# Graph products between the gate products of an LSTM, and a Householder step without z

## What is computed

```python
x = x + L0(h, adj)   # two linear layers with batch norms over all tokens
# L1: two graph convolutions, then four LSTMs with windows of p = 1, 2, 3, 4 nodes
h = relu(einsum('ts,bsh->bth', adj, x @ Wg0 + bg0))
h = relu(einsum('ts,bsh->bth', adj, h @ Wg1 + bg1))
for p in range(1, 5):
    last = lstm_last(Wih[p-1], Whh[p-1], bih[p-1], bhh[p-1], windows of p nodes of h)
    h = h.at[:, idx, :].set(last)      # the last node of each window
# L2: features through the eigenvectors of the 64 x 64 normalized Laplacian
_, U = eigh(L_norm)
out = U @ (relu((U.T @ features) @ W1 + b1) @ W2 + b2)
# L3: three convolutions with adj * adj
```

## Time and profile before

| | us |
|---|---|
| median of 3 runs (lowest, highest) | 1040.38 (1039.38, 1042.43) |
| the profiled execution | 1039.46 |
| its span, first to last instruction | 1037.7 |
| mean granted clock of TensorE | 0.939 |
| busy: PE / PEld / DVE / ACT / POOL | 862.0 / 573.9 / 585.2 / 528.8 / 333.5 |
| chain that ended last, share of the span | PE 57%, DVE 26%, POOL 7%, ACT 6%, issue 3% |

### The profile page before, as it was taken

One profiled execution on the slowest core, in us unless ns is written; L12 is line 12 of the kernel. 1 busy time (PEld: TensorE's weight loads), 2 busy tenths in 40 slices (PEclk: granted clock), 3 DMA queues, 4 the chain that ended last, 5 costly groups with the idle time before them and its releaser, 6 DMA issues.

```text
span 1037.7 us, 12401 instructions
## 1 busy us (share of the span) xinstructions
PE 862.0 (83%) x3721; PEld 573.9 (55%) x3721; DVE 585.2 (56%) x3105; ACT 528.8 (51%) x962; POOL 333.5 (32%) x404
## 2 busy tenths in 40 slices
PE   2678487498879899798857858896899999999998
PEld 1444233353558546684435723575756857857856
DVE  5899867876865877488997886202503303303101
ACT  1466365375464755657526445455545545545531
POOL 1333101016555266525736316674301201201000
PEclk9999889598899999999978889998899999999999
DMA  7000000000000000000000000000000100100101
GB/s 322 0 2 1 0 0 1 1 1 1 1 1 1 1 0 2 1 1 1 0 0 1 1 1 1 1 0 1 1 1 1 41 1 1 42 0 1 42 1 40
DMA packets 2963, 13.32 MB, mean 13 GB/s; under 512 B 465, under 2 KB 465, under 8 KB 2641
## 3 DMA queue, kind: packets, MB, share of 16 engines
q1 hardware_dynamic: 2896, 12.54, 3.0%
HBM read 8.35 MB, written 4.19 MB: 12 GB/s over the span
## 4 chain that ended last, share of the span: by engine, by line
PE 57%; DVE 26%; POOL 7%; ACT 6%; issue 3%; DMA 0%; SPq 0%; DVEq 0%; ACTq 0%; POOLq 0%
PE PS L401 56%; POOL BIG L881 6%; DVE ST L1530 2%; ACT T L784 2%; DVE stats L1502 1%; ACT BIG L823 1%; DVE Fq L1322 1%; DVE seg L1323 1%; ACT T L773 1%; ACT BIG L815 1%; DVE T L1626 1%; DVE mv L1509 1%; POOL sc L861 1%; DVE sc L1063 1%; DVE vcol L1060 1%
## 5 line engine op out<-in xcount | busy, mean ns | idle before, releaser
L401 PE MATMUL PS<-BIG,wts 128*128 128x512 f32 (+2 forms) x1264 | 443.2, 507 | 41.7 <-POOL BIG L881 21.3
L401 PEld LDWEIGHTS PS<-BIG,wts 128*128 128x128 f32 x1264 | 244.4, 198 | 207.4 <-issue 123.7
L881 POOL TENSOR_TENSOR BIG<-BIG 128x256 f32<-128x256 f32 (+2 forms) x272 | 255.3, 944 | 273.2 <-ACT BIG L815 208.0
L815 ACT ACTIVATE BIG<-PS,lbias 128x256 f32<-128x256 f32 (+2 forms) x312 | 166.1, 559 | 125.7 <-PE PS L401 124.6
L1641 DVE TENSOR_TENSOR X<-X,PS 128x512 f32<-128x512 f32 x64 | 43.5, 683 | 148.7 <-PE PS L401 87.1
L722 ACT ACTIVATE BIG<-PS 128x1024 f32<-128x1024 f32 x64 | 65.5, 1024 | 88.5 <-PE PS L401 88.5
L722 ACT ACTIVATE T<-PS 128x512 f32<-128x512 f32 x96 | 55.3, 593 | 100.5 <-PE PS L401 100.3
L730 ACT ACTIVATE T<-X,shift,rstd 128x128 f32<-128x128 f32 x192 | 78.3, 481 | 43.7 <-DVE shift L1518 43.7
L401 PE MATMUL PS<-T,wts 128*128 128x512 f32 x192 | 97.3, 637 | 0.7 <-ACT T L722 0.4
L1663 DVE TENSOR_TENSOR T<-PS,wts 128x512 f32<-128x512 f32 x16 | 11.1, 692 | 150.6 <-PE PS L401 150.6
L869 POOL TENSOR_SCALAR rstd<-mv 128x4 f32<-128x4 f32 x48 | 10.9, 228 | 225.3 <-DVE mv L1509 225.3
(11 more groups left out here) (303 smaller groups left out, 1154.3 us busy)
## 6 DMA issues: line engine op xcount, KB each, us to landing
X<-x_in SPq DMA_DIRECT2D x1, 4096.0 KB, 12.6
...
```

The lines of the kernel that those rows point to most:

```text
L401: return nc.tensor.matmul(o, l, r, start=start, stop=stop)
L815: nc.scalar.activation(LB[:, q, {"i": I_, "g": G_, "f": F_, "o": O_}[g], 0:n], PS[:, 3 * q + rank[q] % 3, 0:n], ACT.Tanh if g == "g" else ...
L881: nc.gpsimd.tensor_tensor(out, a, b, op).then_inc(pool_set[q], 1)
```

## The change

1. In L1 there is no graph stage behind the first one any more. The products of iteration i+1, and the turns of h of iteration i-1, are single tasks between the gate products of iteration i, at places given by the table TASKS (round, set, half): after the second gate, or behind the last. All tasks use one PSUM bank, `task_bank`, and each waits until the one before has been emptied. h has a second tile for odd iterations (H1).
2. bn and norm are cut into pairs of chunks, at rounds 0 and 4 (SCALED, NORMED), ahead of the tanh of the cell. In the last iteration the norm of L2's first chunks stands there (LAST_NORMED), with its statistics and roots.
3. The first LayerNorm of L1 takes its roots on GpSimd, chunk by chunk, and VectorE does it ahead of its first reflection of this part. The last turn of h is done behind the first products of L2, into the odd banks.
4. A reflection forms neither z nor the row sum with the finished v: the row sum is formed with the unfinished v beside the inverse root (ax) and corrected by beta; the factors for the next row and for S come from scalars.
5. The planner's paces are PACE_AV 7.2 (8.0), PACE_GRID 50, 38 (40, 32), PACE_TWIST 32 (27), PACE_SCAN 15 (13). SHORT_ROUND is gone.

The tables:

```diff
+TASKS = {
+    (0, 1, 1): ("turn", 0), (1, 0, 0): ("turn", 1), (1, 0, 1): ("turn", 2), (1, 1, 0): ("turn", 3),
+    (2, 0, 1): ("turn_h", 0), (2, 1, 1): ("turn_h", 1), (3, 0, 0): ("turn_h", 2), (3, 0, 1): ("turn_h", 3),
+    (4, 1, 1): ("agg", 0), (5, 0, 0): ("agg", 1), (5, 0, 1): ("agg", 2), (5, 1, 0): ("agg", 3),
+    (5, 1, 1): ("g0", 0), (6, 0, 0): ("g0", 1), (6, 0, 1): ("g0", 2), (6, 1, 0): ("g0", 3),
+    (6, 1, 1): ("agg2", 0), (7, 0, 1): ("agg2", 1), (7, 1, 1): ("agg2", 2), (8, 0, 0): ("agg2", 3),
+    (8, 0, 1): ("g1", 0), (8, 1, 1): ("g1", 1), (9, 0, 1): ("g1", 2), (9, 1, 1): ("g1", 3),
+}
+NORMED = {(4, 0): (0, 1), (4, 1): (2, 3)}
+SCALED = {(0, 0): (0, 1), (0, 1): (2, 3)}
+LAST_NORMED = {(9, 1): (0, 1), (10, 0): (2, 3)}
+LAST_ROOTS = 7
+DONE_BY = {"turn": "add", "turn_h": "add_h", "agg": "aggT", "g0": "bias0", "agg2": "aggT2", "g1": "bias1"}
...
-PACE_AV = 8.0
-PACE_GRID = [40.0, 32.0]
-PACE_TWIST = 27.0
-PACE_SCAN = 13.0
+PACE_AV = 7.2
+PACE_GRID = [50.0, 38.0]
+PACE_TWIST = 32.0
+PACE_SCAN = 15.0
```

TensorE:

```diff
+            def task(j, name, k):
+                if held[0]:
+                    before, what, c = held[0]
+                    if what in ("agg", "agg2"):
+                        pe.wait_ge(act_done[c], C_ACT.at(before, DONE_BY[what]))
+                    else:
+                        pe.wait_ge(dve_done[c], C_DVE.at(before, DONE_BY[what]))
+                product(j, name, k, task_bank)
+                held[0] = (j, name, k)
...
-                        for g in gates(s):
+                        for at, g in enumerate(gates(s)):
...
                                 pe.wait_ge(act_set[q], R_ACT.at(i, rank[q][m - 3]))
+                            elif i:
+                                pe.wait_ge(act_set[q], R_ACT.at(i - 1, LAST_GATES[m]))
...
                             spend(n * 4 * (2 if s else 1.25) / 2400)
-                        if s == 0 and p > 2:
-                            spend(SHORT_ROUND)
-                        if r and turned < NK and i + 1 < ITER:
-                            turn(i + 1, turned)
-                            turned += 1
-            for k in range(NK):
-                turn(0, k)
-            spend(8.0)
+                            if at == 1 and 0 in todo:
+                                task(*todo[0])
+                        if 1 in todo:
+                            task(*todo[1])
...
+            for name in ["turn"] + GRAPH:
+                for k in range(NK):
+                    if name == "agg":
+                        pe.wait_ge(dve_done[k], C_DVE.at(0, "add"))
+                    product(0, name, k, l1_bank(k))
+                spend(STARTED if name == "turn" else GAP)
...
                 lstm(i)
-                spend(GAP)
-                for k in range(NK):
-                    pe.wait_ge(pool_set[k // 2], R_POOL.start(i + 1))
-                    for t in range(TPC):
-                        j = nc.tensor.transpose(l1_bank(k)[:, t * P:(t + 1) * P],
-                                                by_tile_of_set(k)[:, t, :], ident)
-                    j.then_inc(pe_done[k], 1)
-                    spend(0.5, i, k, "turn_h")
...
                     else:
-                        for c in range(NK):
-                            pe.wait_ge(dve_done[c], C_DVE.end)
+                        for q in range(2):
+                            pe.wait_ge(act_set[q], R_ACT.start(ITER))
                     tiles(bank(k), k, T0[:, k, :], BDU[:, :])
+                if i == 0:
+                    pe.wait_ge(dve_done[NK - 1], C_DVE.end)
+                    for k in range(NK):
+                        product(ITER - 1, "turn_h", k, odd_bank(k))
```

ScalarE:

```diff
                             rank[q] += 1
+                            if at == 0:
+                                for j, name, k in late:
+                                    after(j, name, k, task_bank)
+                                late = []
+                            for half, j, name, k in tasks(i, r, q):
+                                if name in ("agg", "agg2") and at == (2 if half == 0 else len(gates(s)) - 1):
+                                    after(j, name, k, task_bank)
+                        late = [(j, name, k) for _, j, name, k in tasks(i, r, q) if name in ("g0", "g1")]
+                        if i + 1 < ITER:
+                            for k in SCALED.get((r, q), ()):
+                                bn(i + 1, k)
+                            for k in NORMED.get((r, q), ()):
+                                norm(i + 1, k)
+                        else:
+                            for k in LAST_NORMED.get((r, q), ()):
+                                norm_tiles(0, k, "norm", D_DVE.at(0, "shift"), C_PE.at(ITER - 1, "agg2"))
                         act.wait_ge(pool_set[q], R_POOL.at(i, f"c{r}" if s else f"ig{r}"))
                         nc.scalar.activation(LB[:, q, I_, 0:n], LB[:, q, CELL, 0:n], ACT.Tanh).then_inc(act_set[q], 1)
+                assert not late
...
-            for k in range(NK):
-                norm_tiles(0, k, "norm", D_DVE.at(0, "shift"), C_PE.end)
```

The reflection on VectorE:

```diff
-                z = eb(1)[:, 0:NODES - 1 - k]
-                first = op(v.scalar_tensor_tensor(trail, z, vn, trail, ALU.mult, ALU.add))
-                yield
+                first = op(v.scalar_tensor_tensor(trail, eb(2)[:, 0:NODES - 1 - k], vn, trail, ALU.mult, ALU.add))
+                yield first
                 dve.wait_ge(hh_ops, first)
-                op(v.scalar_tensor_tensor(trail, row_of(k, True), zn, trail, ALU.mult, ALU.add))
-                yield
+                yield op(v.scalar_tensor_tensor(trail, row_of(k, True), wc, trail, ALU.mult, ALU.add))
...
-                    op(v.tensor_scalar(sg, x0, 0.0, 2.0, ALU.is_gt, ALU.mult))
+                    sign = op(v.tensor_scalar(sg, x0, 0.0, 2.0, ALU.is_gt, ALU.mult))
                     yield
-                    next(behind, None)
+                    updated = next(behind, None)
                     yield
                     op(v.tensor_tensor_reduce(junks[:, 1, 0:m], vr, ident[:, k + 1:NODES], 1.0, 0.0, ALU.mult, ALU.add, xc))
+                    yield
+                    dve.wait_ge(hh_ops, sign)
+                    op(v.tensor_scalar(sn2, sg, -1.0, n2, ALU.add, ALU.mult))
+                    yield
+                    if updated:
+                        dve.wait_ge(hh_ops, updated)
+                    op(v.tensor_tensor_reduce(junks[:, 3, 0:m], trail, vr, 1.0, 0.0, ALU.mult, ALU.add, ax))
...
-                need(op(v.tensor_scalar(norm, y_, n2, -1.0 / 8192, ALU.mult, ALU.mult)))
-                need(op(v.tensor_scalar(beta, sg, -1.0, norm, ALU.add, ALU.mult)))
-                op(v.tensor_scalar(vcol[:, :], C("next")[:, k:k + 1], beta, xc, ALU.mult, ALU.add))
-                op(v.tensor_scalar(vr[:, 0:1], vr[:, 0:1], beta, None, ALU.add))
+                need(op(v.tensor_scalar(beta, y_, sn2, -1.0 / 8192, ALU.mult, ALU.mult)))
+                v.tensor_scalar(vcol[:, :], C("next")[:, k:k + 1], beta, xc, ALU.mult, ALU.add).then_inc(hh_v, 1)
+                v.tensor_scalar(Av, trail[:, 0:1], beta, ax, ALU.mult, ALU.add).then_inc(hh_v, 1)
                 need(op(v.tensor_scalar(x0, x0, beta, None, ALU.add)))
-                v.tensor_tensor_reduce(junks[:, 3, 0:m], trail, vr, 1.0, 0.0, ALU.mult, ALU.add, S[:, NODES:NODES + 1])\
-                    .then_inc(hh_v, 1)
                 need(op(v.tensor_scalar(hd, x0, beta, guard, ALU.mult, ALU.max)))
                 need(op(v.reciprocal(nc_, hd)))
-                op(v.tensor_scalar(half_nc, nc_, -0.5, None, ALU.mult))
-                op(v.tensor_scalar(a0, x0, nc_, -1.0, ALU.mult, ALU.mult))
-                op(v.tensor_scalar(vn, vcol[:, :], nc_, -1.0, ALU.mult, ALU.mult))
+                dve.wait_ge(hh_v, k + 1 + k + 1 - REFLECTED)
+                first = op(v.tensor_scalar(a0, x0, nc_, -1.0, ALU.mult, ALU.mult))
+                second = op(v.tensor_scalar(vn, vcol[:, :], nc_, -1.0, ALU.mult, ALU.mult))
+                op(v.tensor_scalar(pn, Av, nc_, -1.0, ALU.mult, ALU.mult))
+                need(first)
+                op(v.tensor_scalar(c2, a0, nc_, -1.0, ALU.mult, ALU.mult))
+                need(second)
+                op(v.tensor_scalar(vnn, vn, nc_, -1.0, ALU.mult, ALU.mult))
                 small_product()
                 dve.wait_ge(hh_av, k + 1)
-                dve.wait_ge(hh_v, k + 1)
-                need(hh[0])
-                av = eb(2)[:, 0:m]
-                need(op(v.tensor_scalar(kappa, eb(2)[:, m:m + 1], half_nc, None, ALU.mult)))
-                got = op(v.scalar_tensor_tensor(zrow[:, 0:m], xr, kappa, av, ALU.mult, ALU.add))
-                column = op(v.tensor_scalar(zc, vcol[:, :], kappa, S[:, NODES:NODES + 1], ALU.mult, ALU.add))
+                t = eb(2)[:, m:m + 1]
                 if k + 1 < REFLECTIONS:
+                    got = op(v.tensor_scalar(w0, eb(2)[:, 0:1], nc_, -1.0, ALU.mult, ALU.mult))
+                    need(got - 1)
```

(67 more changed lines are left out.)

231 lines of the change are left out of this document (135 added, 96 removed).

## The result

The changed kernel takes 1001.53 us (median of four runs, 1000.01 to 1002.95), the kernel before 1039.88 (1038.46 to 1042.43) beside it: ratio 0.9628, 95% interval 0.9604 to 0.9652. The forecast was 990 with a range of 968 to 1012. So the change is faster, by 38 us and not by 50. The profiled execution has a span of 999.4 us.

The account below looks back on a forecast made before the run. It took TensorE's queue as the bound and costed each iteration as its work plus expected waits: -0.7 at the start, -39.8 in four stages, -7.5 at the last part's head, -48 in total from 1039.46, giving 990 us, range 968 to 1012.

Parts of the forecast that it names:

- the four stages: LSTM iterations 0 to 3, the last to its last gate: 114.6, 115.7, 107.8 and 105.0 us, together -39.8.
- the head of the last part: Last gate to the end of the next layer's first graph products and late turn: 10.3 us, so -7.5.
- The single bank: Hand-offs of graph-product tasks through one bank: 1 us per iteration with tasks, bounds 0 and 78 us.
- rival D: TensorE stands at each task until the single bank is emptied: slower, 1069 us at 1.09 per task; chance 0.05.
- the norm blocks: ScalarE's norm tiles cut into two blocks: the wait moves and does not go, 5.5 us with the clock.
- rival A: TensorE alone bounds; tasks fill every gap, so hand-off, LayerNorm, transition and unassigned waits vanish: 965 us; chance 0.14.
- A shorter step shortens nothing: Householder: VectorE fits on average, so the 0.3 us saved per reflection gains nothing; 2 us of waits in iterations 0 and 1.
- The second grid is free too: Second grid product: VectorE needs 31.5 + 5 for biases against 38 units, so TensorE does not wait.
- Twist 0.5: Twist product, last LSTM: VectorE needs 36 + 2 of h adds against 33 units and a 3.5 wait: 0.5 us.
- the vectors: Last LSTM: VectorE needs 22 us with the next stage's statistics beside it, against 16 to 18: wait of 4.5.
- The clock: Last LSTM: 2 us for TensorE's lowered clock behind the waits at the vectors and the last product.
- Rival B: VectorE already 88% busy; each LayerNorm 3 us late, biases hold ScalarE, V slips: +20, 1010 us; chance 0.10.

Follow-up runs that it names:

- the honest clock: Changed kernel with VectorE's placing clock counting 0.16 us per grid step, 0.43 per twist step, and wide instructions at their own length: 998.1 us, ratio 0.9575.
- the second trace: The changed kernel itself, unaltered, run again beside the kernel before: 1002.05 us, ratio 0.9613.
- the fastest version: Changed kernel plus the honest clock, LayerNorm instructions at 0.25, GpSimd roots spread, grid paces 52 and 38, twist 42, next-layer shifts after the last eigenvector copy: 972.96 us.

## Why the prediction was right in the large, and where it failed

*Right.* Of the 48 us forecast 38.3 came (spans 1037.7 and 999.4): the start 2.1 and not 0.7, the four stages 27.5 and not 39.8, the head of the last part 8.7 and not 7.5. That the stages missed by only 12 us is in part luck, since errors of 11 and 23 us stood against each other. TensorE's queue was the bound and its work the base of the sum. Filling the rounds took the idle time out of the first two iterations, the longer pace took 10 to 11.5 of the 12.99 us from the first grid, and the head of the last part shrank as forecast: from the last gate (676.0) to the end of the turned hidden states (685.1) it is 9.1 us, against 10.3 forecast and 17.8 before. The first Householder pair did stand ahead of the first graph product, at 201.54 us.

*The single bank.* It cost 1.9 us in iteration 1, about 1.7 in iteration 0 and 2.5 in iteration 2, not the 1.09 per task of rival D's upper bound. The Trainium skill (Perfetto Trace Analysis, Matmuls) asks for groups that rotate through banks, so that the emptying of one overlaps the next. One bank for 72 tasks did not cost an evacuation per task here (0.63 to 0.69 us for an add on VectorE): the gates between two tasks hide most of them. But in iteration 3 one hand-off alone cost 10.29 us, when the add that empties the bank came late. The prediction had named waits at tasks of over 10 us in an iteration as a sign that it is wrong, and there it was; rival D's mechanism was real in that one place. The cause of the late add is its place in VectorE's stream (with the honest clock the wait is gone on the same single bank); whether a second bank would have covered for it no run shows.

*Iterations 0 and 1, 11 us too much.* The terms for waits were too large: 5.5 for the norm blocks with their clock, 0.5 for LayerNorm, 2 for VectorE at the pairs, 2 for transitions, 2 unassigned. I had moved the norm's old wait to its new place nearly whole. Cut in two and with other products to do meanwhile it costs 0.96 us in iteration 1; the 1.37 at 374.05 is the transition to p=3. This was rival A's mechanism, true for the most part in two of the four iterations. In iteration 0 the waits came to 4.4 us, but TensorE was busy for 106.7 with work put at 100.1, at a granted clock of 0.95 (104.1 at 0.98 in the second trace). In iteration 1 it was busy for 1.1 more than was put, at a clock of 1.00, so in iteration 0 the clock, priced at 1.5, took an estimated 3 to 5.

*"A shorter step shortens nothing".* Wrong: it is worth 5 us here. I compared averages (97 us of work in 113), but pairs are spaced evenly and the rest of VectorE's work isn't; that this is the reason is argued from where the waits stand, no run moves that work. The text's own aside, 2 us more of waits if the step saved nothing, was the better half of the thought; the traces show 2.7 at the pairs behind the first, and 0.5 at the first.

*"The second grid is free too".* This step failed. The sum of VectorE's work there was right (36.5 forecast; 47.4 less the 10.3 of idle is 37.1). What I left out is that a bias is a wait for TensorE, and where in the stream it stands is set by a clock I had taken for true. The wait was 8.4 us. The run with the honest clock shows that it goes with the clock, and that it is worth less than its length.

*"Twist 0.5".* Mis-sized twice: VectorE needs 41.5 us and not 38, and the adds stand too late; the second cost 10.3 us at the turn and hid the first. The forecast put 4.5 us at the vectors instead, where 0.5 were lost (1.7 in the second trace).

*The roots on GpSimd* were missing from the sum: 5.3 us of work in the chain, 3.8 of it paid. My list of moved work had the statistics on VectorE and not what GpSimd does with them. The steps of a moved LayerNorm are on three engines.

*The clock* in iteration 3 was priced at 2 us. TensorE was busy for 90.7 us with work that takes 84.9 in the fastest version: 5.8 us. Its granted clock was 0.88 there: 0.50 from 586.8 to 592.0, 0.59 from 608.8 to 613.0 and 0.50 from 648.4 to 653.7, behind the waits of 10.29, 2.07 and 5.70. A small slip beside these: LayerNorm before took 23.2 us and not 22.4, which leaves out the length of its last instruction.

Rival B (VectorE late, 1010) named the right engine and the wrong cause: not the load (101.3 us of 117.8 in iteration 2 and 59.0 of 118.5 in iteration 3, where the fastest version needs 107.5 and 100.2 for the same work), but the place of single instructions, and when TensorE asks. That the waits of iterations 2 and 3 come from orders and paces and not from work is shown by the fastest version. How the 29 us split among the edits is not fully settled, as they overlap.
